# A fused attention and expert network on one core: the first couples' scores by query placed between the halves of the last experts' second layers

## What is computed

```
scores = einsum('bhqd,bhkd->bhqk', q, k) / sqrt(dh)
attn = softmax(scores);  out = einsum('bhqk,bhkd->bhqd', attn, v)
```

## Time and profile before

| | |
|---|---|
| median of three runs | 2785.61 us |
| the profiled execution | 2781.71 us |
| its span, first to last instruction | 2779.5 us |
| PE busy | 2374.3 us, 85% |
| DVE busy | 1534.7 us, 55% |
| ACT busy | 1519.0 us, 55% |
| POOL busy | 550.3 us, 20% |
| mean granted clock of TensorE | 0.924 of 2.4 GHz |

### The profile page before, as it was taken

The page is one execution under the profiler, slowest core; times in us unless marked ns, Lnnn a source line. Parts: engine busy times, 40 slices in busy tenths (PEclk is TensorE's granted clock), DMA queues, the critical chain, the costliest instruction groups (busy, mean ns, idle before and its releaser), DMA issues. The chain is left out here.

```text
span 2779.5 us, 69956 instructions
## 1 busy us (share of the span) xinstructions
PE 2374.3 (85%) x27712; PEld 1658.1 (60%) x27712; DVE 1534.7 (55%) x4449; ACT 1519.0 (55%) x2379; POOL 550.3 (20%) x730
## 2 busy tenths in 40 slices
PE   4667899898989899898989889898989889888975
PEld 2445656575756667575756657575756657564643
DVE  4353545656565655656575565656575565634232
ACT  1334555656656665665656565566655665645432
POOL 3111111221212121221212121121212121111111
PEclk9567989999999999999999999999999999998975
DMA  3100101101010101111010101011010101010000
GB/s 114 28 23 19 32 20 29 29 24 33 24 44 24 44 24 29 24 29 33 23 45 24 44 20 33 19 34 33 24 45 24 44 18 35 18 29 17 17 20 17
DMA packets 103752, 84.21 MB, mean 30 GB/s; under 512 B 15000, under 2 KB 102681, under 8 KB 102937
## 3 DMA queue, kind: packets, MB, share of 16 engines
q1 hardware_dynamic: 103449, 79.91, 11.7%
HBM read 14.21 MB, written 4.19 MB: 7 GB/s over the span
## 5 line engine op out<-in xcount | busy, mean ns | idle before, releaser
L1019 DVE TENSOR_REDUCE smax<-by_query_banks 128x8 f32<-128x616 f32 (+1 forms) x512 | 516.1, 1008 | 350.7 <-PE by_query_banks L1340 350.1
L804 ACT ACTIVATE probs<-by_key_banks 77x1024 f32<-77x1024 f32 (+1 forms) x480 | 485.1, 1011 | 169.1 <-PE by_key_banks L1363 165.4
L1277 PEld LDWEIGHTS by_key_banks<-moe_w,hid 128*128 128x128 f32 x4096 | 476.0, 192 | 14.1
L1277 PE MATMUL by_key_banks<-moe_w,hid 128*128 128x128 f32 x4096 | 483.7, 275 | 0.0
L785 ACT ACTIVATE hid<-by_query_banks,cols 128x512 f32<-128x512 f32 x512 | 334.3, 686 | 262.6 <-PE by_query_banks L1268 260.8
L1411 PE MATMUL weighed_bank<-probs,values 128*32 128x128 f32 x8192 | 366.5, 302 | 5.0 <-ACT o_sb L809 2.7
L1340 PE MATMUL by_query_banks<-k_int,q_int 32*128 32x128 f16 (+1 forms) x4096 | 201.0, 220 | 173.2 <-DVE smax L1019 93.7
L1340 PEld LDWEIGHTS by_query_banks<-k_int,q_int 32*128 32x128 f16 x4096 | 122.4, 99 | 337.2 <-issue 215.4
L1411 PEld LDWEIGHTS weighed_bank<-probs,values 128*32 128x32 f32 x8192 | 211.5, 117 | 99.5 <-issue 48.9
L798 ACT ACTIVATE m_sb<-turned_bank 16x128 f16<-16x128 f32 x256 | 67.6, 264 | 303.8 <-PE turned_bank L1393 303.7
L1363 PE MATMUL by_key_banks<-q_int,k_int 32*128 32x128 f16 x3840 | 211.9, 235 | 5.6 <-ACT probs L804 3.9
(11 more groups left out here) (295 smaller groups left out, 3874.7 us busy)
## 6 DMA issues: line engine op xcount, KB each, us to landing
q_int<-q_nat SPq DMA_DIRECT2D x256, 128.0 KB, 2.7
k_int<-k_nat SPq DMA_DIRECT2D x128, 128.0 KB, 2.7
k_int<-k_nat SPq DMA_DIRECT2D x128, 77.0 KB, 2.3
x_tok<-in_x SPq DMA_DIRECT2D x17, 256.0 KB, 3.0
q_int<-m_sb SPq DMA_DIRECT2D x256, 4.0 KB
out<-res SPq DMA_DIRECT2D x16, 256.0 KB, 2.6
ctx_tok<-in_ctx SPq DMA_DIRECT2D x17, 154.0 KB
hid<-in_moe_w SPq DMA_DIRECT2D x1, 2048.0 KB
```

The costliest lines, as they stand in the source:

```text
L804: act.activation(probs[h % 2][0:nk], pair[0:nk], ACT.Exp, scale=DH ** -0.5)\
L1019: dve.tensor_reduce(smax[h // 2 % 2][:, pair, :], scores, AX.X, ALU.max, negate=True)\
L1277: last = pe.matmul(B[e % 2][:, seq_tok(b)], hidden[e % 2][:, c, seq_tok(b)], moe_w2[:, e, c, :], start=(c == 0), stop=(c == CHUNKS - 1))
```

## The change

The stream HEAVY gets another order. Behind `out6_0` stands `score1_0`, behind `out6_1` `score1_1`, behind `out7_0` `score1_2` and `max1_0`, and behind `out7_1` the rest of the heads as before. So that the experts and the heads can alternate, the function `heavy` of PE, ACT and DVE is split in two streams, `expert_phases` and `heavy`. The strings of PE, ACT, DVE and SP have their letters moved. In the turns with experts no engine's other phases change places among themselves, but on PE `sa_turn`, `proj0` and `query0` now all stand between `score1_2` and `max1_0`, and on DVE `sa_hat` stands between the reductions of c1 and c2, ahead of the sum of expert 7. In the turn before the first with experts, PE has `score1_2` ahead of `hidden0` instead of behind it.

```
-HEAVY = [*experts(), *(phase for phase, _, _, _ in heads_of(PASS))]
+def in_heavy_order():
+
+    first_heads = (phase for phase, _, _, _ in heads_of(PASS))
+    for phase in experts():
+        yield phase
+        if phase in (f"out{EXPERTS - 2}_0", f"out{EXPERTS - 2}_1"):
+            yield next(first_heads)
+        elif phase == f"out{EXPERTS - 1}_0":
+            yield next(first_heads)
+            yield next(first_heads)
+    yield from first_heads
+
+
+HEAVY = list(in_heavy_order())
...
 TURNS = {
-    "PE": "iiiiiihxlhhxxxllhlhllhhllhxlhlhllhhxhhlhhllxhhhlhlhhllhhlllhhhhxxxhhhhhhxhxhxhhhhhhxhhhhhhhhhhxh"
+    "PE": "iiiiiihxlhhxxxllhlhllhhllhxlhlhllhhxhhlhhllxhhhlhlhhllhhlllhhhhxxxhhhhhhhxxxhhhhhhhxhhhhhhhhhhxh"
...
-    "DVE": "lllxhhxhhhhxxxlllllllilhhhhxllhhhhhhhhilllllhhhhlllhhhhlxxxhhhhhhxxhhhhhhhhxhhxxxhhhhhhhhhhhhhhh"
+    "DVE": "lllxhhxhhhhxxxlllllllilhhhhxllhhhhhhhhilllllhhhhlllhhhhlxxxhhhhhhhhxxhhhhhhxhhxxxhhhhhhhhhhhhhhh"
...
-            def heavy(r):
+            def expert_phases(r):
                 if r.b:
                     g = r.b
                     for e in range(EXPERTS):
...
+
+            def heavy(r):
                 for phase, kind, m, h in heads_of(PASS):
...
             def go(r):
-                weave(turn_of(r, "ACT"), heavy(r), light(r), *([layers(r)] if r.n else []), *([inputs(r.i)] if r.i else []))
+                weave(turn_of(r, "ACT"), expert_phases(r), heavy(r), light(r), *([layers(r)] if r.n else []), *([inputs(r.i)] if r.i else []))
...
-            def heavy(r):
+            def expert_phases(r):
 
-                a_free, b_free, o_free, z_free = [None, None], [None, None], None, None
+                a_free, b_free = [None, None], [None, None]
                 if r.f or r.t:
                     p = r.heads[None]
                     a_free = [("smax", p, COUPLES)] * 2
                     b_free = [("probs", p, COUPLES)] * 2
-                    o_free, z_free = ("o_sb", p, BLOCKS), ("o_norm", p, BLOCKS)
...
+            def heavy(r):
+
+                a_free, b_free, o_free, z_free = [None, None], [None, None], None, None
+                if r.f or r.t:
+                    p = r.heads[None]
+                    a_free = [("smax", p, COUPLES)] * 2
+                    b_free = [("probs", p, COUPLES)] * 2
+                    o_free, z_free = ("o_sb", p, BLOCKS), ("o_norm", p, BLOCKS)
+                if r.b:
+                    g = r.b
                     a_free = [("gelu", g, 31), ("gelu", g, 32)]
                     b_free = [("moe_acc", g, 8), ("moe_acc", g, 9)]
```

More of the change, by code:

```diff
@@ L119 @@
 TURNS = {
-    "PE": "iiiiiihxlhhxxxllhlhllhhllhxlhlhllhhxhhlhhllxhhhlhlhhllhhlllhhhhxxxhhhhhhxhxhxhhhhhhxhhhhhhhhhhxh"
+    "PE": "iiiiiihxlhhxxxllhlhllhhllhxlhlhllhhxhhlhhllxhhhlhlhhllhhlllhhhhxxxhhhhhhhxxxhhhhhhhxhhhhhhhhhhxh"
           "hhhhhhhxhhhhhhhhxhhhhhhhhxhhhhhhhhxhhhhhhxxxhhhhhhhhhhhhhhhxhhhhhhhhhhhxxhhhhhxhxxxhhhhhhhhhhhhh"
           "hhxhhhhxhhhhxxxxhhhxxxhhhhhhhhhhxhhxxxxh",
-    "ACT": "iiiihxxxxhhllllhhhhllllhxlhhhlllhxhhhllhlllhhhhhhhxlllllhhhhhhhhhhhhhiixxxxxhhhxhhhhxhhhhhhhhhhh"
+    "ACT": "iiiihxxxxhhllllhhhhllllhxlhhhlllhxhhhllhlllhhhhhhhxlllllhhhhhhhhhhhhiixxxxxhhhhxhhhhxhhhhhhhhhhh"
           "xhhhhhhhhxhhhhhhhhhhxhhhhhhxhhhhhhhhxxxxhhhhhhhhhhhhhhhhhhhhhhhhxxhhhhhhhhhhhhxxxxxhhhhhhhhhhhhh"
           "hhhxhhhhxxxxhhhxxxxhhhhhhhhhhhhhhxxhhxxx",
-    "DVE": "lllxhhxhhhhxxxlllllllilhhhhxllhhhhhhhhilllllhhhhlllhhhhlxxxhhhhhhxxhhhhhhhhxhhxxxhhhhhhhhhhhhhhh"
+    "DVE": "lllxhhxhhhhxxxlllllllilhhhhxllhhhhhhhhilllllhhhhlllhhhhlxxxhhhhhhhhxxhhhhhhxhhxxxhhhhhhhhhhhhhhh"
           "hhhhhhhhxhhhhhhhhxxxhhhhhhhhhhhhhhhhhhhhxxhhhhhhhhxhhhhhhhhhhhhxhhhhxhhhhxxhhhhxxhhhhhhhhxxxhhhh"
@@ L131 @@
           "xxixxxxxxxxxiiiixxxxxxxxxxxxxxxxxxxxxxxi",
-    "SP": "iiiiiillllllxxxxxhhhhhhhhhhhhhhhhhhhhhhhhhhhhhhhhhhhhllllllllllllllllxxxxxxhhhxhhhhhhhhhhhxxxhhh"
+    "SP": "iiiiiillllllxxxxxhhhhhhhhhhhhhhhhhhhhhhhhhhhhhhhhhhhllllllllllllllllxxxxxxhhhhxhhhhhhhhhhhxxxhhh"
           "hhhhhhhhhhhhhhhhhhhhhhhhhhhhhxxxxxxxxxxxxxxxxxxxhhhhhhhhhhhhhhhhhhhhhhhhhhhhhhhhhhhhhhhhhhhhhhhh"
@@ L137 @@
           "hxhhhhhihhxhhhhhihhhhxhxxhxxhhxxxxxxxxhh",
-    "early ACT": "hhhlhxhlhhhlhlhhhhlhxxhhhhhxhlhhhlhhhhxhlllhhhlhhxhhhhhhhhlhlhhhlllhhhllhhhhlhhhxhhhhhlhhhhihhhh"
+    "early ACT": "hhhlhxhlhhhlhlhhhhlhxxhhhhhxhlhhhlhhhhxhlllhhhhlhhhxhhhhhhlhlhhhlllhhhllhhhhlhhhxhhhhhlhhhhihhhh"
           "hlxhhhhhhhlxihhhhhhxxxxxxxhxhhxhhhhxxhxhhhhhhhhhxhhhhhhhhhhhhhxhhhhhiihhhhhhhhxxhhhhhhhhxxhhhxhi"
@@ L146 @@
           "hxhhhhhhhxhxxhxxxhxxxhhxhxhhhhhhhhhhhihh",
-    "early SP": "hhhhhhhhhxhhhhhhhhhhhlhhhhhxhhhhhlhhlxhlhhhxxllhhhhlhhxhhhhhlhlhlhlllhhhhxhhhlhllhhhxllllhlhhxhh"
+    "early SP": "hhhhhhhhhxhhhhhhhhhhhlhhhhhxhhhhhlhhhhlxhlxxllhhhhhlhhxhhhhhlhlhlhlllhhhhxhhhlhllhhhxllllhlhhxhh"
           "lihhhhxhhhxhhhxxxxxhxxhhhhxxhihhhxhhhhhhxhhhxxhhhhhxhhhhhhhhhhihihhxxhhxhhhxxhhhhxhhhhxxhxhhhhhh"
@@ L1144, in go @@
             def go(r):
-                weave(turn_of(r, "DVE"), heavy(r), light(r), *([layers(r)] if r.n else []), *([inputs(r.i)] if r.i else []))
+                weave(turn_of(r, "DVE"), expert_phases(r), heavy(r), light(r), *([layers(r)] if r.n else []), *([inputs(r.i)] if r.i else []))
             alone(inputs(Group(0)))
@@ L1533, in go @@
             def go(r):
-                weave(turn_of(r, "PE"), heavy(r), light(r), *([layers(r)] if r.n else []))
+                weave(turn_of(r, "PE"), expert_phases(r), heavy(r), light(r), *([layers(r)] if r.n else []))
             pe.wait_ge(s_first, first_in)
```

## The result

The changed kernel takes 2807.73 us (median of four runs, 2807.05 to 2808.11). Four runs of the kernel before, interleaved with them, took 2784.03 us (2782.11 to 2786.24). The ratio is 1.0091, with a 95% interval of 1.0073 to 1.0110: slower by 23.7 us, where I had forecast 16.6 and said 2802. The profiled execution took 2807.76 us.

What follows compares the result with a forecast made beforehand. The prediction took PE's work plus the stalls in its queue as the bound. Its terms, 18.8 - 2.9 + 0.7 = 16.6 us, gave a median of 2802 us, with an 8-in-10 range of 2787 to 2816.

Steps and rivals of the forecast that it cites:

- c1 without a stall: On PE, the second couple of heads starts at 3.87 us from the first half without its former 1.17 us stall.
- sa_turn wants the hat: a new stall of 0.85: On PE behind c2, sa_turn waits 0.85 us for DVE's hat, which now has reduction 1 before it.
- proj0 wants feat: a new stall of 0.87: On PE, proj0 directly behind sa_turn waits 0.87 us for ACT's feat.
- c4: a stall of 1.83: On PE behind c3, c4 waits 1.83 us for reduction 3, behind sum 7 on DVE; formerly 0.99.
- c5 at 15.91: c5 starts 15.91 us after the first half instead of 14.57; each of 14 turns 1.34 us longer, 18.8 in all.
- The fifteenth turn: In the turn without light steps, c5 comes at 11.50 us instead of 14.40: 2.9 us less, once.
- The early turn: Before the first turn with experts, hidden0 behind c2 on PE comes up to 1.4 us later; 0.7 taken.
- The clock: TensorE's clock keeps falling behind c5, costing 2.3 us in a turn that falls; no change counted, the main doubt.
- All clear if PE's busy time is the same: Condition for reading the predicted stalls and ways to c5 in the profile after: PE's busy time unchanged.
- Rival (1): Every filled stall gains: hat done by 6.20 instead of 7.0, light steps cost no waits; 2766 us, chance 5%.
- Rival (2): Clock fall behind c5 absent or shorter in seven more turns, giving back 16 us; time stays at 2786, chance 15%.
- Rival (3): Clock falls sooner, behind the new 0.85 and 0.87 stalls, slowing query0 and out7_1 by 2.6 us a turn; 2820, 12%.

Runs made afterwards that it cites:

- x_hat: The changed kernel with the vector engine's hat run behind reduction 0, ahead of the sum of expert 6: 2788.9 us, ratio 1.0026 to the kernel before.
- x_sum: The changed kernel with the vector engine's sum of expert 7 behind reduction 3, ahead of reduction 4: 2787.4 us, ratio 1.0025 to the kernel before.
- x_again: The changed kernel run again, unedited: 2804.1 us, ratio 1.0069 to the kernel before.
- x_early: The changed kernel with hidden0 back ahead of c2 in the turn before the experts: 2803.4 us, ratio 1.0071 to the kernel before.
- the pads: The kernel before with one or two chunks of expert 5's first layer computed twice: 2790.1 and 2798.9 us, ratios 1.0025 and 1.0063.
- x_cover: The changed kernel with proj0 and query0 on TensorE behind c3, ahead of c4 (ScalarE's proj0 behind max1_0): 2737.6 us, ratio 0.9836 to the kernel before.
- x_best2: The changed kernel with x_early's, x_hat's and x_sum's edits, proj0 behind c3 and query0 behind c4: 2727.3 us, ratio 0.9790 to the kernel before.
- x_group: The kernel before, halves left together, with only sa_turn, proj0 and query0 put together behind c2 on TensorE: 2850.9 us, ratio 1.0245.
- x_proj: The changed kernel with proj0 and query0 on TensorE behind out7_1, ahead of c3 (ScalarE's proj0 behind max1_0): 2777.8 us, ratio 0.9992 to the kernel before.

## Why the prediction was right, and where it was off

The direction, the mechanism and the order of size were right, by the steps as they were put, and the 2807.7 us lie 5.7 above the 2802 said; each step with what it measured, in the turn of the earlier trace rows:

- c1 without a stall, c0 to c2 under the halves: so it is. The cost of splitting the halves was not in the sum. Behind a half and ahead of the next there were 1.88, 1.99, 1.98 and 1.88 us instead of 1.81 each: 0.49 us in all for changing between the fp32 halves and the couples.
- "sa_turn wants the hat: a new stall of 0.85": it was 0.55 by the row, 0.62 from the end of c2's 0.25 us in PE's queue, which is how the 0.85 was counted. The hat ended 0.17 us later than worked out, but c2 came 0.40 later, for the reason above. x_hat removed just this stall and won 0.62.
- "proj0 wants feat: a new stall of 0.87": 0.87, 14 times more.
- "c4: a stall of 1.83": 1.85. x_sum took the sum away from in front of the reduction and c4 waited 0.99 again.
- From proj0 to max1_0, 2.02 was taken and 1.82 measured, and from there to out7_1 0.21 and 0.11; from c3 to c4 2.08 and 2.17. The two shorter steps and the shorter hat stall, 0.53 us, pay for the halves. So c5 at 15.91 (15.94 measured): that the sum hit within 0.03 us is luck, since its terms erred both ways. 14 turns: 18.8 forecast, 19.3 measured.
- The fifteenth turn: -2.9 forecast, -2.5 measured on the way to c5; the split halves again.
- The early turn: 0.7 forecast. From c0 there to POOL's next root it was 8.20 us before (133.59 to 141.79), 8.90 with the change (134.19 to 143.09) and in x_again, and 8.20 again in x_early: 0.7. The 2.0 us by which the first turn starts later are more than that, but lie inside the 4.7 us by which kernels of the same order differ there.
- The clock: "I expect the fall to stay, and count nothing for it". Behind c5 that held to 0.2 us. What failed is the assumption that nothing has to be counted for the clock elsewhere: five turns have a late fall instead of one, which, less the three falls some 48 us in that are gone, makes 5.0 us in the profiled execution, and the fifteenth turn lost 2.1. The runs don't settle why. By the pads turn length alone costs no more than some 2.5 us; that the pattern shifts with each small change is seen in every row of the table.
- "All clear if PE's busy time is the same": it was not, PE was busy 15.1 us longer. The halves' 0.49 us make 7 of these in 14 turns; the low clock lasted longer both in the 14 turns (171 us instead of 157) and in the fifteenth, and goes with the rest.

The terms of work sum to 19.3 + 0.7 - 2.5 = 17.5 us, against a loss of 23.7 and 23.0 in two comparisons of medians, 25.3 and 19.2 by their ratios. So 2 to 8 us are left. The traces put them down to the clock, mostly to the late falls, but one execution's pattern alone can be 7 us off either way, as the pads' traces are.

Rival (1) needed the hat done before c2; it was not. In x_hat it was, and the waits for feat (0.87) and of c4 (1.85) stayed, so this one point did not decide it. Still x_cover shows that the stretch had more to win than I gave it: not the 1.17 us of c1, but 1.48 us of way against before in x_cover and 2.53 in x_best2. With it x_cover won 1.7 us of clock behind c5 in each turn (190.6 less 166.9, by 14) and lost 0.6 of it again in the rest of the turn (8.7 us, by 14). My sentence that only 1.17 of the 2.81 us can be reached was wrong, since I held the light steps' places for given. Rival (2), the clock giving back, did not happen with the change but did in x_cover. Rival (3) did not happen with the change either, and happened in x_group.

## What to carry to other kernels

When independent work is put between steps of a chain, look at what the moved steps had been covering: a chain turn, copy, project needs something between each pair, and steps put next to one another lose it. Place small steps one by one into the waits that the trace shows, behind the step that starts the other engine's part; here that took the kernel from 0.9% over to 2.1% under. And where the clock falls behind a thin stretch, price the filling of that stretch with the clock, not with the stalls alone.

## What was not expected of the hardware

- The granted clock fell behind stalls of no more than 1.2 us between small matmuls (0.99 and 0.65 ahead of c5), and cost up to 2.4 us a turn. It is not bound to: behind the same stretch it fell in 12 of the 14 turns before and stayed up in two, that of the earlier trace rows among them. With the last of these at 0.69 but two dense pairs ahead of it, it stayed up (x_cover).
- A half of an expert's second layer (16 matmul passes, 1.81 us among other halves) takes 0.07 us longer with a couple behind it alone, and 0.17 to 0.18 longer with couples on both sides.
- With every instruction's order fixed, executions of one kernel differ by up to 1.1% (x_proj 2767.8 to 2799.4 us; the longest had a mean clock of 0.886, the nine others, 2767.8 to 2781.1 us, one of 0.923 to 0.931). The two traces of the changed kernel, after and x_again, have their five late falls in turns that are only in part the same. Its first four runs alone would have given its time as known to 1 us; the next five ranged over 18 us.
